# The second normalisation of a block pipeline: scale and shift on ScalarE, modulation in whole-block products on VectorE

## The reference, cut to what matters

```python
def _layernorm(x, axis=-1, eps=1e-05):
    m = jnp.mean(x, axis=axis, keepdims=True)
    v = jnp.var(x, axis=axis, keepdims=True)
    return (x - m) / jnp.sqrt(v + eps)
...
mod = (_silu(L0_c) @ L0_wmod).reshape(L0_c.shape[0], 6, 1, -1)
sa, ca, ga, sb, cb, gb = (mod[:, 0], mod[:, 1], mod[:, 2], mod[:, 3], mod[:, 4], mod[:, 5])
...
h = _layernorm(x, axis=-1) * (1 + ca) + sa
x = x + ga * _L0_attn_ref(h, ...)
h = _layernorm(x, axis=-1) * (1 + cb) + sb
x = x + gb * _L0_ffn_ref(h, ...)
```

## Time and profile before

| | |
|---|---|
| median of 3 runs | 587.58 us (587.25 to 587.61) |
| the profiled execution | 584.68 us |
| its span | 582.5 us |
| mean granted clock of TensorE | 0.954 |
| busy: PE, VectorE (DVE), ScalarE (ACT), POOL | 544.5, 473.1, 302.2, 282.8 us |

### The profile page before, as it was taken

The page is one execution under the profiler, slowest core; times in us unless marked ns, Lnnn a source line. Parts: engine busy times, 40 slices in busy tenths (PEclk is TensorE's granted clock), DMA queues, the critical chain, the costliest instruction groups (busy, mean ns, idle before and its releaser), DMA issues.

```text
span 582.5 us, 13330 instructions
## 1 busy us (share of the span) xinstructions
PE 544.5 (93%) x4008; PEld 404.8 (69%) x4009; DVE 473.1 (81%) x1062; ACT 302.2 (52%) x514; POOL 282.8 (49%) x197
## 2 busy tenths in 40 slices
PE   9999999999999985779899999999999999999992
PEld 5544555655656552537588888888888888888881
DVE  1267889999999989999688888888888888888882
ACT  4777688889797863654433333333333333333330
POOL 0004033343423342000638878877878877777634
PEclk9988999999899987858899999999999999999997
DMA  8314544644735437833677897786886686786533
GB/s 313 126 45 155 153 136 109 203 132 136 208 103 176 115 120 219 309 64 70 162 121 107 136 152 118 136 132 116 145 157 109 134 139 121 136 155 112 88 45 36
DMA packets 82109, 79.37 MB, mean 136 GB/s; under 512 B 45140, under 2 KB 71892, under 8 KB 81816
## 3 DMA queue, kind: packets, MB, share of 16 engines
q0 software_dynamic: 16912, 31.74, 31.3%
q1 hardware_dynamic: 63864, 46.28, 29.9%
q10 hardware_dynamic: 1296, 0.87, 0.5%
HBM read 44.06 MB, written 22.23 MB: 114 GB/s over the span
## 4 chain that ended last, share of the span: by engine, by line
PE 72%; DVE 13%; ACT 4%; issue 4%; DMA 4%; POOL 2%; POOLq 0%; DVEq 0%; ACTq 0%
PE ps L807 30%; PE ps L826 14%; PE ps L551 13%; PE ps L610 3%; DMA out_rows<-w_stage,region 3%; PE ps L652 2%; PE ps L564 2%; PE ps L648 2%; PE ps L474 1%; DVE region L1293 1%; POOL out_rows L1749 1%; ACT region L976 1%; PE ps L482 1%; ACT region L923 1%; DVE region L1415 1%
## 5 line engine op out<-in xcount | busy, mean ns | idle before, releaser
L807 PE MATMUL ps<-region,w_sb 128*128 128x256 f16 (+1 forms) x1920 | 194.3, 261 | 0.9 <-DMA region<-region 0.4
L807 PEld LDWEIGHTS ps<-region,w_sb 128*128 x1920 | 170.4, 98 | 20.1 <-issue 2.1
L1749 POOL DMA_INDIRECT out_rows<-w_stage,region x71 | 126.4, 1780 | 60.4 <-DMA out_rows<-w_stage,region 22.8
L1739 POOL DMA_INDIRECT region<-h_scratch,region x71 | 91.8, 1292 | 67.7 <-DVE region L1576 45.0
L1178 ACT ACTIVATE region<-region 128x1024 f16<-128x1024 f32 (+1 forms) x40 | 38.5, 961 | 130.4 <-DVE region L1630 130.4
L826 PE MATMUL ps<-region 128*128 x852 | 99.6, 273 | 1.9 <-DVE region L1636 1.7
L1622 DVE TENSOR_SCALAR region<-ps,region 128x256 f32<-128x256 f32 (+1 forms) x160 | 64.4, 448 | 43.0 <-PE ps L807 41.2
L826 PEld LDWEIGHTS ps<-region 128*128 128x128 f16 x852 | 82.6, 98 | 13.1 <-issue 3.5
L1166 ACT ACTIVATE region<-ps,region 128x256 f32<-128x256 f32 (+1 forms) x160 | 63.0, 445 | 53.0 <-PE ps L807 49.5
L551 PE MATMUL ps<-region 128*128 128x512 f32 x192 | 84.2, 595 | 3.2 <-ACT region L923 3.2
L1723 POOL TENSOR_TENSOR region<-region 128x512 f32<-128x512 f32 x30 | 37.3, 1270 | 94.9 <-DVE region L1320 94.9
(11 more groups left out here) (238 smaller groups left out, 702.3 us busy)
## 6 DMA issues: line engine op xcount, KB each, us to landing
w_stage<-in_w SPq DMA_DIRECT2D x20, 512.0 KB, 3.7
region<-in_x SPq DMA_DIRECT2D x8, 512.0 KB, 7.3
out_rows<-region SPq DMA_DIRECT2D x8, 512.0 KB, 3.0
h_scratch<-gb_bc SPq DMA_DIRECT2D x4, 1024.0 KB, 6.8
h_scratch<-region SPq DMA_DIRECT2D x8, 512.0 KB, 3.2
region<-region POOLq DMA_DIRECT2D x7, 512.0 KB, 4.5
region<-in_ramp SPq DMA_DIRECT2D x1, 2064.0 KB, 11.1
region<-in_w SPq DMA_DIRECT2D x4, 512.0 KB, 6.6
```

The source lines that it names most:

```text
L807: mm = pe.matmul(ps[:, GV + 2 * half + a, (f % 2) * MT:(f % 2) * MT + wide], w, xg_t[:, s, xa * KD + k, 0:wide], start=(n == 0), stop=(n = ...
L1739: G.indirect_dma_start(out=xg_rows[:, t % XG, u, :], out_offset=None, in_=h_scratch, in_offset=bass.IndirectOffsetOnAxis(ap=idx, axis=0)). ...
L1749: G.indirect_dma_start(out=out, out_offset=bass.IndirectOffsetOnAxis(ap=scatter_idx[:, at:at + 1], axis=0), in_=y_sb[:, t % 2, u, :], in_o ...
```

## The change

The scale and shift by r and -m * r of the second normalisation go to ScalarE, in place in `x2`, four activations per block (`rows2`), placed between the gates and `normal_rows`. The reciprocal moves forward on VectorE into `ln2_scale`, ahead of the Nyquist column, with one new 128x4 instruction that forms the shift -m * r. `ln2_rows` becomes one product and one sum over the whole block (128x1024), the modulation rows broadcast. The wait for the DMA of `x2` moves from VectorE to ScalarE. The square root `std2` moves, in passes 1 to 6, ahead of `gate_rows`. The counts of `h2_ready` go from four to one per block.

```diff
--- before.py
+++ after.py
@@ -205,6 +205,7 @@
         ny_run = carve(2 * TPB + 1)
         ny_g = carve(TPB)
         shift1 = carve(2 * TPB).rearrange("p (s j) -> p s j", s=2)
+        shift2 = carve(TPB)
         eps_col = carve(1)
         eps_unit = carve(1)
 
@@ -330,6 +331,7 @@
                              "l_gate l_gates").split())
         w_in = sems("w_in", 4)
         unit_set = sem("unit_set")
+        ln2_shift, ln2_rows_in = sem("ln2_shift"), sem("ln2_rows_in")
         iota_in, gb_in = sem("iota_in"), sem("gb_in")
         w_lo = sems("w_lo", 2)
         lo_mm, w_hi, gate_split, h2_hi, h2_lo, hid_hi, y_mid = (sem(n) for n in (
@@ -968,6 +970,13 @@
                 nc.scalar.activation(mag[:, t % 2, VAL, :], mag[:, t % 2, VAL, :], ACT.Identity,
                                      bias=eps_unit).then_inc(eps_ready, 1)
 
+            def rows2(t):
+                act.wait_ge(ln2_shift, t + 1)
+                act.wait_ge(x2_out, 16 * (t + 1))
+                for j in range(TPB):
+                    nc.scalar.activation(x2[:, j, :], x2[:, j, :], ACT.Identity, bias=shift2[:, j:j + 1],
+                                         scale=rstd[:, 2, j:j + 1]).then_inc(ln2_rows_in, 1)
+
             def gate_rows(t):
                 for k in range(KD):
                     act.wait_ge(tp2_done, KD * t + k + 1)
@@ -991,7 +1000,7 @@
 
             def split_rows(t):
 
-                act.wait_ge(h2_ready, TPB * (t + 1))
+                act.wait_ge(h2_ready, t + 1)
                 if t == 0:
                     act.wait_ge(mod_out, 16)
                 if t >= 1:
@@ -1002,7 +1011,7 @@
             def split_weights(n):
                 act.wait_ge(w_in[stage_of(n)], 16 * arrivals(n))
                 if n in (18, 19):
-                    act.wait_ge(h2_ready, TPB * LAST)
+                    act.wait_ge(h2_ready, LAST)
                 elif n >= W1_CHUNKS:
                     act.wait_ge(idft_done, min(n // 2 - 1, NBLK))
                 nc.scalar.activation(parts_of(n)[HI], staged(n), ACT.Copy, scale=SW).then_inc(w_hi, 1)
@@ -1107,15 +1116,19 @@
                     split_weights(4)
                     split_weights(5)
                     continue
+                if 1 <= t < LAST:
+                    std2(t - 1)
                 if t >= 2:
                     gate_rows(t - 2)
                 if t >= 1 and t + 2 < NBLK:
                     project(t + 2)
-                if t >= 1:
+                if t == LAST:
                     std2(t - 1)
                 low_piece(t + 1, 1)
                 if t >= 2:
                     gate(t - 2)
+                if t >= 1:
+                    rows2(t - 1)
                 if t >= 1 and t + 2 < NBLK:
                     normal_rows(t + 2)
                 if t >= 1:
@@ -1423,19 +1436,21 @@
                 done(V.memset(picked[:, :, 0:1], 0.0), V.tensor_scalar(pcol1[:, 0:1], pcol, 1.0, None, ALU.add))
                 picks(0, C1, picked, keep, ahead).then_inc(early_ready, 1)
 
+            def ln2_scale(t):
+                dve.wait_ge(ln2_std, t + 1)
+                V.reciprocal(rstd[:, 2, :], rstd[:, 2, :]).then_inc(ln2_rstd, 1)
+                dve.wait_ge(ln2_rstd, t + 1)
+                V.scalar_tensor_tensor(out=shift2, in0=mv[:, 1, :, 0], scalar=-1.0, in1=rstd[:, 2, :], op0=ALU.mult,
+                                       op1=ALU.mult).then_inc(ln2_shift, 1)
+
             def ln2_rows(t):
                 b = t // 2
-                dve.wait_ge(ln2_std, t + 1)
-                V.reciprocal(rstd[:, 2, :], rstd[:, 2, :]).then_inc(ln2_rstd, 1)
-                dve.wait_ge(x2_out, 16 * (t + 1))
-                for j in range(TPB):
-                    V.scalar_tensor_tensor(out=x2[:, j, :], in0=x2[:, j, :], scalar=mv[:, 1, j, 0:1],
-                                           in1=mod_bc[:, b, 2, :], op0=ALU.subtract, op1=ALU.mult).then_inc(h2_mid, 1)
-                dve.wait_ge(ln2_rstd, t + 1)
-                for j in range(TPB):
-                    dve.wait_ge(h2_mid, TPB * t + j + 1)
-                    V.scalar_tensor_tensor(out=x2[:, j, :], in0=x2[:, j, :], scalar=rstd[:, 2, j:j + 1],
-                                           in1=mod_bc[:, b, 1, :], op0=ALU.mult, op1=ALU.add).then_inc(h2_ready, 1)
+                dve.wait_ge(ln2_rows_in, TPB * (t + 1))
+                V.tensor_tensor(x2, x2, mod_bc[:, b, 2, :].unsqueeze(1).to_broadcast([P, TPB, D]),
+                                ALU.mult).then_inc(h2_mid, 1)
+                dve.wait_ge(h2_mid, t + 1)
+                V.tensor_tensor(x2, x2, mod_bc[:, b, 1, :].unsqueeze(1).to_broadcast([P, TPB, D]),
+                                ALU.add).then_inc(h2_ready, 1)
 
             ln1_moments(0)
             ln1_rows(0)
@@ -1452,6 +1467,8 @@
                 if t >= 3:
                     top2(t - 3)
                 if 0 <= t < NBLK:
+                    if t >= 1:
+                        ln2_scale(t - 1)
                     nyquist_apply(t)
                     if t + 2 < NBLK:
                         ln1_rows(t + 2)
```

## The result

The changed kernel took **597.55 us** (median of 4 runs, 594.79 to 600.03) against 587.41 for the kernel before: ratio 1.0172, with a 95% interval of 1.012 to 1.0223. The forecast of 595.1 was right in sign and about right in size.

The account below looks back on a forecast made before the run. The prediction took a ring of TensorE and ScalarE, without VectorE, to bound each pass. +8.5 in passes 1 to 5 and -1.0 in the tail gave +7.5: 592.2 for the profiled execution, 595.1 us as median, range 590 to 601.

Parts of the forecast that it names:

- Four rows on ScalarE, +8.5: Passes 1 to 5: four activations of 1.99 us per pass, 9.95, less 1.3 idle and 0.16 slack, delay TensorE by 8.5 us.
- idle time of 1.3 us: ScalarE's idle time before L909, summed over four passes, waiting for VectorE's small shift; the new rows were to fill it.
- VectorE, -0.4 a block, worth nothing in passes 1 to 5: VectorE saves 0.7 us per block less 0.3 for small operations; in passes 1 to 5 this is only idle time.
- The waits costed at nothing: ScalarE's added waits, for the square root's moments, the shift and the DMA of x2, were to cost nothing.
- 0.9 us of lead: VectorE was to run 0.9 us earlier against TensorE in passes 1 to 5, covering the waits added on ScalarE.
- a sign of being wrong: The prediction listed the new rows waiting for the shift or the DMA of x2 among signs against it.
- The tail, -1.0: Last block: bind starts 0.6 us earlier, small operations cost 0.3, VectorE's shorter rows give 0.7; 1.0 us gained.
- VectorE as the bound: Rival: VectorE is the real bound, TensorE's delay vanishes at L652, each of seven blocks gains 0.4; 584.8 us, chance 0.08.
- Only the first pass pays: Rival: ScalarE makes up the time behind its waits for TensorE, one 1.8 us stays; 588.4 us, chance 0.07.
- The clock falls more often: Rival: new waits idle TensorE and its clock drops; three falls more give 598.7 us, five 601; chance 0.15.
- price of 1.2 us: The prediction's cost for one fall of TensorE's clock, from pass 4's 21.51 us against pass 3's 20.35.
- The shift comes only when POOL is done: Rival: rows start where L909 starts now, 1.3 us of idle time goes unused; +8.8, 596.4 us, chance 0.10.

Follow-up runs that it names:

- half_rows: The changed kernel with two of the four rows per block on ScalarE and the other two on VectorE; 594.23 us, ratio 1.0083 to the kernel before.
- rows_left_out: The changed kernel without the four ScalarE activations per block, all else kept; 587.98 us, ratio 0.9996 to the kernel before.
- nyquist_row_first: The changed kernel with the four new ScalarE rows moved, in passes 1 to 5, behind the Nyquist row; 594.16 us, ratio 1.01 to the kernel before.
- rows_last_two: The kernel before with the new form only for blocks 5 and 6 (passes 6 and 7); 588.99 us, ratio 1.001 to the kernel before.
- vector_short: The kernel before with four of VectorE's eight row instructions per block left out; 587.06 us, ratio 0.9991 to the kernel before.
- no_low_halves: The changed kernel with POOL's subtraction for the low halves replaced by a fill with zero; 596.7 us, ratio 1.0115 to the kernel before.
- changed_again: The changed kernel run once more, unaltered, in a second comparison; 596.29 us against 588.38 for the kernel before, ratio 1.0154.
- rows_first_five: The changed kernel with the new form only for blocks 0 to 4 (passes 1 to 5), the old form after; 596.67 us, ratio 1.0157 to the kernel before.

## Why the prediction was right, and where it was wrong

**Four rows on ScalarE, +8.5.** Right: 1.98 us for four, passes 3 and 5 of 27.0 (26.8 forecast), +8.63 and +8.53 over five passes in two executions. half_rows and rows_left_out show that it is the rows, nyquist_row_first that it is also their place. The composition differs, and that the sum came out is in part luck. A pass lengthened by the rows' 1.98 us, less what they started ahead of L909's old start. That was 0.23 us in pass 1 and 0.35 in pass 2, and nothing in passes 3 and 5: in pass 3 the rows start 17.68 us after the transform (136.44 - 118.76), and L909 started 17.65 after it before (132.78 - 115.13). So of the idle time of 1.3 us that I subtracted 0.6 was used. Pass 4 made up for most of the rest. The kernel before had a fall of the clock there and the changed one had none, which is worth 0.6 (26.10 against 25.48 in rows_last_two); I had put 0.16 for this pass.

**VectorE, -0.4 a block, worth nothing in passes 1 to 5.** Right: the pair took 2.48 (2.5), VectorE waited 1.10 for the roots. vector_short shows that even 1.6 us would have bought nothing.

**The waits costed at nothing.** Right for the DMA of x2: it ends no idle time before L977 in passes 1 to 5. Not quite for the square root. Timeline of VectorE's moments and of ScalarE in the changed kernel, pass 2:

```profile
105.97 0.38 DVE L1275 BATCH_NORM_AGGREGATE region<-region 128x2 f32<-128x6 f32 x4
...
106.38 0.30 ACT L961 ACTIVATE region<-region 128x4 f32<-128x4 f32 x1
106.59 1.92 ACT L985 ACTIVATE region<-ps 128x1024 f16<-128x1024 f16 x2
```

The root (L961) starts 0.03 us after the moments end, and the transposes behind it (L985) 14.89 us after the transform (106.59 - 91.70), where they started after 14.44 before; the gates come 0.4 later for it (109.36 - 91.70 = 17.66, before 106.93 - 89.67 = 17.26). In passes 3 and 5 the moments are there in time, and the root only puts the transposes off by 0.2 (14.63 against 14.44). Half wrong for the shift: I gave VectorE 0.9 us of lead. It had 1.36, since bind starts 2.63 us ahead of the next transform (118.76 - 116.13) and not 1.27 (115.13 - 113.86), and POOL took it back with the 1.35 at L1308. In pass 4 the rows waited for the shift, which the prediction had named as a sign of being wrong. The chain of waits through the changed kernel, pass 3 (start us, us, what):

```profile
135.71 0.71 DVE region L1443
...
138.42 2.06 ACT region L911 x4
140.48 0.47 ACT region L1077
140.95 1.39 ACT region L968
...
142.37 0.73 ACT region L970
...
143.13 0.71 DVE region L1298
```

Before, the chain ran through TensorE's transform, with L909 in it let go by a shift that ended with POOL's products. Now, in passes 3 to 5, it runs from the shift through ScalarE's queue into bind and round VectorE again, and takes 27.0 in passes 3 and 5 where TensorE's would take 26.8 (no_low_halves).

**The tail, -1.0.** Wrong. Bind of the last block came 0.8 earlier against the transform (223.57 - 200.19 = 23.4, before 215.46 - 191.25 = 24.2; -0.6 forecast), but the step "From there VectorE is the path, up to its last rows" stops too soon. ScalarE's tail in the changed kernel:

```profile
245.27 1.06 ACT L1009 ACTIVATE region<-region 128x1024 f16<-128x1024 f32 x1 [0.79 <-DVE region L1452]
247.52 0.60 ACT L1038 ACTIVATE region<-ps 128x512 f32<-128x512 f32 x1 [1.20 <-PE ps L654]
```

TensorE's last inverse was late next, beginning at half clock: 1.06 us for each of its first three groups from 243.31, 0.59 from 246.45. In rows_last_two the whole inverse took 6.3 us (235.02 to 241.33), before 5.5 (234.91 to 240.44). Up to the last block's gate products (ends 251.18 before, 259.39 in changed_again, +8.2) the tail gave 0.3, and the entry then took 1.7, which the sum had no term for: 8.5 - 0.3 + 1.7 = +9.9, where the spans differ by 592.3 - 582.5 = 9.8. Whether the 1.7 counts in the medians isn't known, since the entry of the kernel before was seen in one execution alone.

**The rivals.** *VectorE as the bound* falls: the time rose, and vector_short gained nothing. The Trainium skill, "Perfetto Trace Analysis", section "Optimizing Scalar/DVE Operations", says that offloading from a saturated VectorE to ScalarE may make sense. Here VectorE was without idle time between two binds and the offload still lost 1.7%, so that sign did not decide. *Only the first pass pays* falls: every pass does. *The clock falls more often* falls for passes 1 to 6 of the changed kernel, which was granted 1.00 throughout in both profiled executions; but rows_first_five, the same in passes 1 to 5, had two falls there, so this was not the new form's doing. The price of 1.2 us set pass 4 against pass 3; against pass 2 it is 0.7 (21.51 and 110.47 - 89.67 = 20.80). A fall that I had not named came at the experts' entry. *The shift comes only when POOL is done* had 0.10 and is what passes 3 to 5 show: the rows start with the end of POOL's products, where L909 started at full clock, and its idle time is not used. That made 27.0 of 26.8, and 27.43 in pass 4, where the rows waited 0.26 for the shift. No run frees the shift from POOL alone; nearest comes no_low_halves, whose shift was over at 163.17 in pass 4, ahead of the gates at 163.87. Passes 1 and 2 went by the forecast's account: in pass 2 the shift was over at 108.56, ahead of the gates (109.36). This rival's 596.4 is nearer to both medians (597.55, 596.29) than 595.1. The rule that I cited with it stands in the Trainium skill, "SBUF — State Buffer", section "SBUF: two separate sides". It agrees with the trace at a second place: L1308 has two SBUF inputs and ends 0.55 us after POOL's subtraction, and 0.70 is its length without it. I had looked for that rule at the shift alone.

**The range and the noise.** The lower end is 595.1 - 2.0 - 2.4 = 590.7 and not 590.5, which 590 covers. That 0.2% could be told from no change was too bold: the intervals of the ratios are 0.3 to 0.5% to either side, and executions of the kernel before lie between 584.24 and 593.21 us.

## What to carry to other kernels

Busy shares did not tell which engine could take more work: ScalarE was at 52% and paid for nearly every microsecond, VectorE at 81% and gave back nothing. Ask whether the place in the engine's queue lies between two things that the bounding engine waits for. There, idle time is room only if the new work does not wait for what the old work waited for; here both waited for a small VectorE instruction that ended with POOL's products. Cost a tail to the point where the next stage starts, with the engine that is late next and its clock: here a gain of 0.7 us ahead of a stage was less than the 1.7 that the clock took at its entry.

## What the runs showed of the hardware that was not expected

- Falls of TensorE's granted clock move between passes and kernels. One cost 0.6 to 1.1 us of a pass: 26.10 (before) against 25.48 (rows_last_two) in pass 4, 26.09 (rows_last_two) against 25.01 (before) in pass 3, and 27.98 (rows_first_five) against 27.00 (changed) in pass 3. Windows of rows_first_five, in pass 2 and across the end of pass 4 and pass 5:

```profile
90.00:115.00 25.00, 23.01 (x110) 13.28 (x111) 22.55 (x36) 21.34 (x35) 10.10 (x8) 0.93 0.57 166
...
167.00:192.00 25.00, 22.11 (x118) 13.47 (x118) 23.44 (x49) 21.45 (x34) 7.98 (x6) 1.00 0.44 129
```

  TensorE was busy 23.01 of 25 us in the stretch with the fall and 22.11 in that without, but a fall itself lengthens the busy time: over the whole of pass 2 it was 25.80 us in rows_first_five and 24.30 in the changed kernel, at full clock, for the same work. The kernel before ran pass 4 with a fall and the changed kernel, with more idle time on TensorE in every pass, with none. What decides it stays open.
- Nine idle products ahead of the experts' entry went with the short entry (3.77 to 3.78) in all three kernels that had them; of the ten profiled executions without them one had it.
